# Two gated attention and expert layers on one core: the first layer taken batch by batch, with the rows for the experts scattered in four groups

## The chip, the cores and the metric

The kernel runs on one core of a Trainium2 chip, as one program. The metric is the device time of one execution in microseconds (us), the median of several. All times in this document are microseconds unless another unit stands beside them. Engines: PE (TensorE, matrix multiplies and transposes), DVE (VectorE), ACT (ScalarE), POOL (GpSimd, which here also issues the indirect DMAs), SP (which issues the plain DMAs).

## The reference, cut to what matters

`x` is 4 batches of 256 tokens with 256 features, `ctx` the same tokens with 64 features. Four steps each add a gated term to `x`; `ln` is a layernorm without weights.

```
sim  = (ctx Wq0)(ctx Wk0)^T scaled; keep the 76 largest of each row     # per batch 256 x 256
A    = sigmoid(sim) * kept;  A = (A + A^T) / 2
x   += tanh(g_xattn[0]) * ((1 - gamma) * ln(x) + gamma * A)             # layer 0, attention
y    = for each token t, expert e = t mod 4 (64 tokens of a batch each):
       (silu(ln(x) Wg_e) * (ln(x) Wu_e)) Wd_e                           # 256 -> 256 -> 256
x   += tanh(g_ffn[0]) * y                                               # layer 0, FFN
s    = (ctx Wq1 + bq)(ctx Wk1 + bk)^T / 8 * ln(x); masks; softmax
x   += tanh(g_xattn[1]) * softmax(s)                                    # layer 1, attention
p    = softmax(ln(x) router), 8 best of 64 experts for each token
x   += tanh(g_ffn[1]) * sum over the 8 of weight * expert(ln(x))        # 256 -> 96 -> 256
```

## The kernel before, in words

Everything is float32. A tile is 128 tokens; a batch is two tiles, the whole input eight. Each engine runs its own program in the order in which it is written, and waits on semaphores for the others.

**Up to the first layer.** PE transposes `ctx`, projects it and makes `sim` for all batches. DVE's `keep_top(b)` finds the 76th largest of each row by ten rounds of `max` (8 values, L991) and `match_replace` (L995), two tiles at a time, and masks `adj` (L1000). `mix_adjacencies(b)` (L1016, L1020) adds the transposed `adj` and the input, `statistics(n, b)` (L966 to L972) makes mean and variance. POOL's `inverse_deviation(n, b)` (L439, L441) turns a variance into 1/sqrt and a shift; ACT's `normalise` (L827) applies them; PE's `transpose_normed` (L583) transposes the result, and ACT's `evacuate_xnt` copies it to `xn_t`.

**FFN of layer 0.** It is done in two halves of two batches. `q` counts half and expert, 0 to 7, each with `TE` = 128 tokens of one expert: `expert_gate_up0(q)` (L604) fills a PSUM bank with gate and another with up, ACT makes `silu0` (L847) and copies `up0` (L849), POOL multiplies them into `h0_t` (L449, `up_times_silu`), `expert_down0(q)` (L593) multiplies by the down weights, ACT copies to `y0_t` (L839), PE transposes it back (`transpose_y0`, L615) and DVE's `add_layer0` adds it.

**Layer 1 up to the experts.** DVE's `masked_scores`, ACT's `exp_scores` (L855), DVE's `add_softmax` and `statistics(3, b)`, POOL's deviation, ACT's normalise into `x_rows`, PE's transposes and `router_logits` (L626), ACT's copy, DVE's `choose_experts` (L1066 to L1072), PE's `rank_rows` (L672, L673: how many earlier tokens chose the same expert) and DVE's `place_rows` (L1080 to L1092), which writes for each token and pick the row in DRAM where its features go (`place_at`).

**Scatter.** POOL then sends the rows: 64 indirect DMAs (L478, `place_rows` in POOL's program), each 128 rows of 320 floats to `expert_rows`, 16 for each batch. They wait for `place_ready` of the batch, for `x_rows_ready`, and for `rows_cleared`: SP's one DMA that fills the first 192 rows of each expert with an empty row (L349). SP loads the expert rows (`load_rows`, L361) only when all 64 have landed (`placed`).

**Experts.** 63 times PE transposes the rows of an expert (L704), multiplies by gate and up (L715) and by down (L724), with DVE and ACT between; POOL scatters the results to `token_picks` (L499). At the end PE sums each token's eight picks (L770) and DVE adds them (L1241). SP loads the experts' weights (L355, L356) eight ahead, the first of them after the last scores, since the weights share a buffer with the projections. Ahead of the experts DVE also counts, lists the experts with over 192 tokens (L1157 to L1186), makes the router weights and picks them (L1113).

**Order.** The eight PSUM banks are taken in turn. `fills` lists every use; `begin(i)` makes PE wait until use `i - 8` was emptied, and `filled(i)` makes a reader wait for `bank_filled`, which counts uses in that order. So the order of all work is written out by hand in five places: the list of fills and the four engines' programs. In the order before, DVE takes `keep_top(1)`, batches 0 and 1 mixed, `keep_top(2)`, 2 mixed, `keep_top(3)`, 3 mixed, then layer 0 and the scores of batches 0 and 1, their experts and places, and last the same for 2 and 3. POOL takes all eight products and most deviations ahead of the first scatter:

```python
            place_rows(0, 0, 2)
            inverse_deviation(2, 2)
            place_rows(0, 2, 4)
            inverse_deviation(2, 3)
            place_rows(0, 4, 10)
            inverse_deviation(3, 2)
            place_rows(0, 10, 13)
            inverse_deviation(3, 3)
            place_rows(0, 13, PICKS)
            for b in range(1, B):
                place_rows(b, 0, PICKS)
```

Of the kernel before, what the change touches and what calls it, by code (L numbers as in the profile page):

```python
# [14 lines left out]
P = 128  # L15
# [19 lines left out]
def gated_layers_kernel(nc, x, ctx_in, mask_ss, mask_bs, g_xattn, g_ffn, wq0, wk0, gamma_raw, gate_up, down,  # L35
# [12 lines left out]
    TE = HALF // NE0  # L48
# [17 lines left out]
    with ExitStack() as stack:  # L66
# [118 lines left out]
        evac = {who: sem(who + "_evac") for who in ("act", "dve")}  # L185
# [35 lines left out]
        F_CTX, F_PROJ, F_SIM, F_SCORE = {}, {}, {}, {}  # L221
        F_CTX[0] = add_fill("ctx", "act")
# [9 lines left out]
        for b in range(B):  # L232
            F_SCORE[b] = add_fill("score", "act")


        F_ADJT, F_XNT, F_YT, F_XNT2, F_LOGIT = {}, {}, {}, {}, {}
        F_GATE, F_UP, F_DOWN = {}, {}, {}

        def add_gate_up_fills(q):
            F_GATE[q], F_UP[q] = add_fill("gate", "act"), add_fill("up", "act")  # L240

        def add_down_fill(q):
            F_DOWN[q] = add_fill("down", "act")

        for fill, name, who in ((F_ADJT, "adjt", "dve"), (F_XNT, "xnt", "act")):
            for b in (0, 1):
                fill[b] = add_fill(name, who)
        for q in range(NE0):
            if q == NE0 - 1:
                F_ADJT[2] = add_fill("adjt", "dve")  # L250
            add_gate_up_fills(q)
            if q:
                add_down_fill(q - 1)
        add_down_fill(NE0 - 1)
        F_XNT[2] = add_fill("xnt", "act")
        F_ADJT[3] = add_fill("adjt", "dve")
        F_YT[0], F_YT[1] = add_fill("yt", "dve"), add_fill("yt", "dve")
        F_XNT[3] = add_fill("xnt", "act")
        add_gate_up_fills(NE0)
        for q in range(NE0 + 1, 2 * NE0 - 1):  # L260
            add_gate_up_fills(q)
            add_down_fill(q - 1)
        F_XNT2[0], F_XNT2[1] = add_fill("xnt2", "act"), add_fill("xnt2", "act")
        add_gate_up_fills(2 * NE0 - 1)
        F_LOGIT[0], F_LOGIT[1] = add_fill("logit", "act"), add_fill("logit", "act")
        add_down_fill(2 * NE0 - 2)
        add_down_fill(2 * NE0 - 1)
        F_RANK = {}
        F_RANK[0], F_RANK[1] = add_fill("rank", "dve"), add_fill("rank", "dve")
        F_YT[2], F_YT[3] = add_fill("yt", "dve"), add_fill("yt", "dve")  # L270
        F_XNT2[2], F_LOGIT[2] = add_fill("xnt2", "act"), add_fill("logit", "act")
        F_XNT2[3] = add_fill("xnt2", "act")
        F_RANK[2] = add_fill("rank", "dve")
        F_LOGIT[3] = add_fill("logit", "act")
        F_RANK[3] = add_fill("rank", "dve")
# [13 lines left out]
        LAYERNORMS = ((0, None), (1, 0), (1, 1), (1, 2), (1, 3), (2, 0), (2, 1), (3, 0), (3, 1), (2, 2), (2, 3), (3, 2), (3, 3))  # L289
# [11 lines left out]
        def xn_t_view(k, b, permuted):  # L301

            if permuted:
                return xn_t[:, k].rearrange("p (f e b g) -> p f e b g", f=2, e=NE0, b=B // 2)[:, b // 2, :, b % 2, :]
            return xn_t[:, k, b * S:(b + 1) * S]
# [99 lines left out]
        def _(pool):  # L405
# [37 lines left out]
            def up_times_silu(half, experts):  # L443
                for e in experts:
                    q = half * NE0 + e
                    emptied(pool, F_UP[q])
                    if q >= 2:
                        pool.wait_ge(bank_filled, F_DOWN[q - 2] + 1)
                    pool.tensor_tensor(h0_t[:, q % 2].rearrange("p i t -> p (i t)"), silu0[:, q % 2], up0[:, q % 2],  # L449
                                       ALU.mult).then_inc(h0_ready, 1)  # L450
# [7 lines left out]
            inverse_deviation(1, 0)  # L458
            inverse_deviation(1, 1)
            up_times_silu(0, range(NE0))  # L460
            for n, b in ((1, 2), (1, 3), (2, 0), (2, 1)):
                inverse_deviation(n, b)
            up_times_silu(1, (0,))
            inverse_deviation(3, 0)
            up_times_silu(1, (1,))
            inverse_deviation(3, 1)
            up_times_silu(1, (2, 3))
# [14 lines left out]
            place_rows(0, 0, 2)  # L482
            inverse_deviation(2, 2)
            place_rows(0, 2, 4)
            inverse_deviation(2, 3)
            place_rows(0, 4, 10)
            inverse_deviation(3, 2)
            place_rows(0, 10, 13)
            inverse_deviation(3, 3)
            place_rows(0, 13, PICKS)  # L490
            for b in range(1, B):
                place_rows(b, 0, PICKS)
# [21 lines left out]
        def _(pe):  # L514
# [49 lines left out]
            for b in range(B):  # L564
                query_times_key(1, F_SCORE, b)

# [20 lines left out]
            def expert_down0(q):  # L587
                i = F_DOWN[q]
                begin(i)
                pe.wait_ge(h0_ready, q + 1)  # L590
                for hc in range(KC):
                    for ic in range(IC):
                        last = pe.matmul(bank(i)[:, hc * TE:(hc + 1) * TE], down_w[:, q % NE0, ic, hc * P:(hc + 1) * P],  # L593
                                         h0_t[:, q % 2, ic, :], start=ic == 0, stop=ic == IC - 1)
                last.then_inc(bank_filled, 1)

            def expert_gate_up0(q):
                half, e = q // NE0, q % NE0
                for part, fill in enumerate((F_GATE[q], F_UP[q])):
                    begin(fill)  # L600
                    for ic in range(IC):
                        for k in range(KC):
                            c = part * I0 + ic * P
                            last = pe.matmul(bank(fill)[:, ic * TE:(ic + 1) * TE], gu_w[:, e, k, c:c + P],  # L604
                                             xn_t[:, k, half * HALF + e * TE:half * HALF + (e + 1) * TE], start=k == 0, stop=k == KC - 1)
                    last.then_inc(bank_filled, 1)

            def transpose_y0(b):
                emptied(pe, F_DOWN[b // 2 * NE0 + NE0 - 1])
# [20 lines left out]
            transpose_adj(0)  # L630
            transpose_adj(1)
            transpose_normed(F_XNT, xn, xn_ready, 0)
            transpose_normed(F_XNT, xn, xn_ready, 1)
            pe.wait_ge(ld["gu"], 16 * NE0)
            pe.wait_ge(ld["down"], 16 * NE0)
            emptied(pe, F_XNT[1])
            for q in range(NE0):
                if q == NE0 - 1:
                    transpose_adj(2)
                expert_gate_up0(q)  # L640
                if q:
                    expert_down0(q - 1)
            expert_down0(NE0 - 1)
            transpose_normed(F_XNT, xn, xn_ready, 2)
            transpose_adj(3)
            transpose_y0(0)
            transpose_y0(1)
# [3 lines left out]
            for q in range(NE0 + 1, 2 * NE0 - 1):  # L651
                expert_gate_up0(q)
                expert_down0(q - 1)
# [623 lines left out]
```

## Time and profile before

| what | value |
|---|---|
| median of three runs | 417.0 (415.72 to 417.07) |
| the profiled execution, its own time | 417.87 |
| its span, first to last instruction | 416.1 |
| mean granted clock of PE | 0.844 of full speed |
| PE, DVE, ACT, POOL busy | 275.1, 210.7, 118.0, 214.0 |

The span has three stages: the two layers up to the places, with the row scatters at their end, to 203.4; the experts from 206.5 to 365.6; the sum of the picks from 383.0 on. Averages of busy time mix these, so the stages must be read one by one. In the timeline a line merges alike instructions that follow each other; the brackets at its end give the idle time before it and what ended it.

### The profile page before, as it was taken

Reading aid. Unit: us, or ns where it says so; the run is one execution under the profiler, and the core shown is the slowest. Engines: PE = TensorE matmul, PEld = TensorE weight load, DVE = VectorE, ACT = ScalarE, POOL = GpSimd, SP = SyncE. Lnnn points to the kernel's source line nnn. Section 1 sums busy time; section 2 is a strip of 40 time slices with the busy share of each in tenths; the row PEclk is TensorE's granted clock in tenths of the full one; section 3 lists DMA queues with packets and bytes.
Section 4 is the critical chain, followed back from the end, with each engine's and each line's share of the span. In section 5 each row is a group of like instructions: output and inputs, shape, how many; then the busy total and the mean of one; then the engine's idle time right before and its main releaser. Section 6 shows DMA issues by size and latency. Waiting matters only on the chain.

```text
span 416.1 us, 5526 instructions
## 1 busy us (share of the span) xinstructions
PE 275.1 (66%) x1546; PEld 230.9 (55%) x1546; DVE 210.7 (51%) x921; ACT 118.0 (28%) x265; POOL 214.0 (51%) x256
## 2 busy tenths in 40 slices
PE   5898177137801610000199999999999999951997
PEld 1335067037800500000189999889999889931886
DVE  0799999989386679000033433343433343340352
ACT  2264353316634500000023333333333333320000
POOL 2622112013267777777327777777777777771000
PEclk9999999557975555555589999999999999995899
DMA  4899995360013333333498888888888887226891
GB/s 132 312 352 306 318 310 192 91 190 2 1 63 113 126 126 127 126 127 138 148 243 267 273 270 277 271 264 274 261 273 269 269 270 229 74 73 234 325 305 64
DMA packets 47374, 84.12 MB, mean 202 GB/s; under 512 B 10453, under 2 KB 28249, under 8 KB 46320
## 3 DMA queue, kind: packets, MB, share of 16 engines
q1 hardware_dynamic: 38128, 64.87, 49.9%
q0 software_dynamic: 9216, 18.90, 13.0%
q8 instruction: 13, 0.21, 0.2%
q14 instruction: 17, 0.14, 0.1%
HBM read 48.07 MB, written 39.85 MB: 211 GB/s over the span
## 4 chain that ended last, share of the span: by engine, by line
PE 52%; DVE 18%; POOL 16%; issue 7%; DMA 4%; ACT 2%; SPq 1%; POOLq 1%; ACTq 0%
PE psum L715 20%; POOL expert_rows L478 14%; PE psum L724 13%; PE psum L770 7%; PE psum L704 5%; DVE work L995 5%; DVE top L991 5%; DVE stats L966 2%; PE psum L536 2%; PE psum L530 2%; DMA sim<-token_picks 1%; POOL token_picks L499 1%; PE psum L604 1%; DVE adj L1000 1%; DMA gu_w<-expert_rows 1%
## 5 line engine op out<-in xcount | busy, mean ns | idle before, releaser
L499 POOL DMA_INDIRECT token_picks<-down_w,target x126 | 117.3, 931 | 54.9 <-issue 41.1
L715 PE MATMUL psum<-gu_w,wgu 128*96 128x192 f32 x504 | 93.7, 329 | 0.0
L715 PEld LDWEIGHTS psum<-gu_w,wgu 128*96 128x96 f32 x504 | 78.0, 165 | 0.6 <-DVE gu_w L1203 0.2
L478 POOL DMA_INDIRECT expert_rows<-x_rows,place_at x64 | 62.4, 975 | 23.8 <-issue 23.8
L724 PE MATMUL psum<-proj_t,gu_w 96*96 96x256 f32 x252 | 64.8, 379 | 0.0
L927 ACT ACTIVATE gu_w<-psum 96x192 f32<-96x192 f32 x63 | 20.6, 326 | 130.0 <-PE psum L715 130.0
L1208 DVE TENSOR_TENSOR gu_w<-gu_w,psum 96x192 f32<-96x192 f32 x63 | 22.1, 350 | 67.1 <-ACT gu_w L927 67.1
L704 PE MATMUL psum<-ident,gu_w 96*128 96x96 f32 x108 | 14.1, 256 | 53.1 <-DMA gu_w<-expert_rows 53.1
L933 ACT COPY down_w<-psum 96x512 f32<-96x512 f32 x63 | 36.6, 581 | 33.9 <-PE psum L724 33.9
L724 PEld LDWEIGHTS psum<-proj_t,gu_w 96*96 96x96 f32 x252 | 41.1, 163 | 7.1 <-DVE gu_w L1208 0.4
L704 PEld LDWEIGHTS psum<-ident,gu_w 96*128 96x128 f32 x108 | 12.5, 148 | 57.6 <-DMA gu_w<-expert_rows 54.4
L1203 DVE COPY gu_w<-psum 128x384 f32<-128x384 f32 x63 | 34.4, 547 | 0.0
L439 POOL TENSOR_TENSOR rstd<-var_eps,minus_half 128x2 f32<-128x2 f32 (+1 forms) x13 | 10.4, 797 | 46.6 <-DVE var_eps L972 46.5
L1202 DVE COPY target<-gu_w 96x2 uint32<-96x2 uint32 x27 | 4.5, 165 | 52.6 <-PE psum L704 52.6
L991 DVE MAX8 top<-work 128x8 f32<-128x256 f32 x72 | 26.8, 413 | 0.0
L995 DVE MATCH_REPLACE8 work<-top,work 128x256 f32<-128x256 f32 x64 | 25.7, 409 | 0.0
L604 PE MATMUL psum<-xn_t,gu_w 128*128 128x128 f32 x128 | 19.0, 316 | 1.7 <-ACT xn_t L832 1.7
L604 PEld LDWEIGHTS psum<-xn_t,gu_w 128*128 128x128 f32 x128 | 18.4, 231 | 2.4 <-issue 1.3
L449 POOL TENSOR_TENSOR h_t<-silu,up 128x256 f32<-128x256 f32 x8 | 6.1, 762 | 23.9 <-ACT up L849 23.6
L770 PE MATMUL psum<-sim,xn_t 128*128 128x256 f32 x32 | 9.9, 480 | 11.0 <-DMA sim<-token_picks 11.0
L1241 DVE TENSOR_TENSOR xs<-psum,scores 128x256 f32<-128x256 f32 x8 | 3.4, 424 | 27.3 <-PE psum L770 27.3
L583 PE MATMUL psum<-ident,x_rows 128*128 128x128 f32 x16 | 3.4, 351 | 20.8 <-ACT x_rows L827 19.8
(177 smaller groups left out, 397.1 us busy)
## 6 DMA issues: line engine op xcount, KB each, us to landing
expert_rows<-empty_rows SPq DMA_DIRECT2D x1, 15360.0 KB, 69.3
wgu<-in_L_ffn_w_gate_up SPq DMA_DIRECT2D x65, 192.0 KB, 2.9
gu_w<-expert_rows SPq DMA_DIRECT2D x28, 240.0 KB, 4.2
proj_t<-in_L_ffn_w_down SPq DMA_DIRECT2D x65, 96.0 KB, 4.0
sim<-expert_rows SPq DMA_DIRECT2D x18, 240.0 KB, 4.3
work<-expert_rows SPq DMA_DIRECT2D x18, 240.0 KB, 4.2
gu_w<-in_L_ffn_gate_up_proj SPq DMA_DIRECT2D x4, 512.0 KB, 8.2
sim<-token_picks SPq DMA_DIRECT2D x2, 1024.0 KB, 4.9
```

Of the source, the lines that this page charges most:

```text
L478: pool.indirect_dma_start(rows_dram, bass.IndirectOffsetOnAxis(ap=place_at[:, t, k:k + 1], axis=0), x_rows[:, t, :], None).then_inc(placed ...
L499: pool.indirect_dma_start(picks_dram, bass.IndirectOffsetOnAxis(ap=target[0:SLOTS, e % T_RING, i:i + 1], axis=0), y_slots[0:SLOTS, n, i, : ...
L604: last = pe.matmul(bank(fill)[:, ic * TE:(ic + 1) * TE], gu_w[:, e, k, c:c + P], xn_t[:, k, half * HALF + e * TE:half * HALF + (e + 1) * T ...
L704: last = pe.transpose(psum[:, e % 2, k * CAP + i * SLOTS:k * CAP + (i + 1) * SLOTS], x_slots[n][0:SLOTS, i, k * P:(k + 1) * P], ident[0:SL ...
L715: last = pe.matmul(psum[0:I1, 2 + e % 2, part * CAP:(part + 1) * CAP], wgu[:, n, k, part * I1:(part + 1) * I1], x_slots_t[:, e % 2, k, :], ...
L724: last = pe.matmul(psum[0:SLOTS, 4 + e % 2, i * D:(i + 1) * D], h1_t[:, e % 2, i * SLOTS:(i + 1) * SLOTS], wd[:, n, :], start=True, stop=True)
L770: last = pe.matmul(psum[:, t, 0:D], diag[:, t % 2, k, :], picks[t % K_RING][:, k * D:(k + 1) * D], start=k == 0, stop=k == TOP_K_EXPERTS - 1)
L933: act.copy(y_slots[0:SLOTS, n].rearrange("p i d -> p (i d)"), psum[0:SLOTS, 4 + e % 2, 0:SUBS * D]).then_inc(y_ready, 1)
L991: dve.max(top8[:, t, r], (work if r else sim)[:, t]).then_inc(top8_ready, 1)
L995: dve.match_replace(work[:, t], top8[:, t, r], (work if r else sim)[:, t], REMOVED).then_inc(rest_ready, 1)
L1203: dve.tensor_copy(x_slots_t[:, e % 2].rearrange("p k n -> p (k n)"), psum[:, e % 2, 0:KC * CAP]).then_inc(xt_copied, 1)
L1208: dve.tensor_tensor(h1_t[:, e % 2], silu1[:, e % 2], psum[0:I1, 2 + e % 2, CAP:2 * CAP], ALU.mult).then_inc(h_ready, 1)
```

## The change

The first layer and what follows it is taken batch by batch. `TE` becomes 64: a product, a gate and up and a down are those of one expert in one batch, so there are 16 of each, and gate and up share one PSUM bank, as the four downs of a batch do. `keep_top` of later batches is cut into rounds and spread between the work of earlier batches. The scores of layer 1 are made later, and each kind of bank has an evacuation semaphore of its own. POOL scatters the rows of batch 0 when they are placed, then those of batch 1, 2 and 3, and does deviations and half of the products between them. The product of silu and up stays on POOL throughout. The parts of the diff that set the order:

```diff
-    TE = HALF // NE0
+    TE = S // NE0
...
+        add_fills(("adjt", 0), ("score", 0), ("score", 1), ("xnt", 0), ("score", 2),
+                  ("gu", 0), ("gu", 1), ("gu", 2), ("adjt", 1), ("gu", 3), ("down", 0),
+                  ("score", 3), ("yt", 0), ("xnt", 1),
+                  ("gu", 4), ("gu", 5), ("gu", 6), ("gu", 7), ("down", 1),
+                  ("xnt2", 0), ("logit", 0), ("yt", 1), ("adjt", 2), ("rank", 0), ("xnt", 2),
+                  ("gu", 8), ("gu", 9), ("gu", 10), ("gu", 11), ("down", 2),
+                  ("xnt2", 1), ("logit", 1), ("yt", 2), ("rank", 1), ("adjt", 3), ("xnt", 3),
+                  ("gu", 12), ("gu", 13), ("xnt2", 2), ("gu", 14), ("logit", 2), ("gu", 15), ("rank", 2), ("down", 3),
+                  ("yt", 3), ("xnt2", 3), ("logit", 3), ("rank", 3))
...
+            def up_times_silu(*which):
+                for q in which:
+                    emptied(pool, F_GU[q])
+                    need(pool, down_step, q - 1)
                     pool.tensor_tensor(h0_t[:, q % 2].rearrange("p i t -> p (i t)"), silu0[:, q % 2], up0[:, q % 2],
                                        ALU.mult).then_inc(h0_ready, 1)
...
             inverse_deviation(1, 0)
+            up_times_silu(0, 1, 2, 3)
             inverse_deviation(1, 1)
+            inverse_deviation(2, 0)
+            up_times_silu(4, 5, 6, 7)
             inverse_deviation(3, 0)
+            inverse_deviation(1, 2)
...
             place_rows(0, 0, 2)
+            inverse_deviation(2, 1)
+            place_rows(0, 2, 9)
+            inverse_deviation(3, 1)
+            up_times_silu(8)
+            place_rows(0, 9, 10)
+            up_times_silu(9)
+            place_rows(0, 10, 12)
+            up_times_silu(10)
+            place_rows(0, 12, 14)
+            up_times_silu(11)
+            place_rows(0, 14, PICKS)
+            place_rows(1, 0, 3)
+            inverse_deviation(1, 3)
+            place_rows(1, 3, 5)
             inverse_deviation(2, 2)
+            place_rows(1, 5, 10)
+            inverse_deviation(3, 2)
+            place_rows(1, 10, 11)
+            up_times_silu(12)
+            place_rows(1, 11, 12)
+            up_times_silu(13)
+            place_rows(1, 12, 14)
+            up_times_silu(14)
+            place_rows(1, 14, PICKS)
+            up_times_silu(15)
+            place_rows(2, 0, 3)
             inverse_deviation(2, 3)
+            place_rows(2, 3, 9)
             inverse_deviation(3, 3)
+            place_rows(2, 9, PICKS)
+            place_rows(3, 0, PICKS)
```

PE takes its work in the order of the fills, with `expert_down0` between: `expert_gate_up0(8)`, `(9)`, `expert_down0(8)`, `expert_gate_up0(10)`, `expert_down0(9)`, `expert_gate_up0(11)`, `expert_down0(10)`, `expert_down0(11)`, and the like for the other batches. DVE's new order, and ACT's from batch 0's products on:

```diff
+            keep_top(1, 0, 2)
+            mix_adjacencies(0)
+            statistics(1, 0)
+            keep_top(1, 2, ROUNDS)
+            keep_top(2, 0, 1)
+            mix_adjacencies(1)
+            statistics(1, 1)
+            keep_top(2, 1, 4)
+            add_layer0(0)
+            statistics(2, 0)
+            keep_top(2, 4, 5)
+            masked_scores(0)
+            keep_top(2, 5, 7)
+            softmax_and_statistics(0)
+            keep_top(2, 7, ROUNDS)
+            choose_experts(0)
             mix_adjacencies(2)
             statistics(1, 2)
+            place_rows(0)
+            add_layer0(1)
+            statistics(2, 1)
+            keep_top(3, 0, 1)
+            masked_scores(1)
+            keep_top(3, 1, 2)
+            softmax_and_statistics(1)
+            keep_top(3, 2, 3)
+            keep_top(3, 3, 4)
+            keep_top(3, 4, 6)
+            choose_experts(1)
+            keep_top(3, 6, 7)
+            place_rows(1)
+            keep_top(3, 7, ROUNDS)
+            add_layer0(2)
             mix_adjacencies(3)
             statistics(1, 3)
+            statistics(2, 2)
             masked_scores(2)
+            softmax_and_statistics(2)
+            router_weights(0)
+            router_weights(1)
+            choose_experts(2)
+            place_rows(2)
+            add_layer0(3)
+            statistics(2, 3)
             masked_scores(3)
+            softmax_and_statistics(3)
             choose_experts(3)
             place_rows(3)
...
+            silu_and_up0(0, 1, 2, 3)
+            normalise(1, 1)
+            evacuate_down(0)
+            copy_scaled(scores, F_SCORE, 3, SCORE_SCALE)
+            evacuate_xnt(F_XNT, True, 1)
+            silu_and_up0(4, 5)
             act.preload_act_table(ACT.Exp)
             exp_scores(0)
+            act.preload_act_table(ACT.Silu)
+            silu_and_up0(6, 7)
+            scale_x(2)
+            evacuate_down(1)
+            normalise(3, 0)
+            evacuate_xnt(F_XNT2, False, 0)
+            copy_logits(0)
+            scale_x(3)
+            normalise(1, 2)
+            evacuate_xnt(F_XNT, True, 2)
+            silu_and_up0(8, 9)
+            act.preload_act_table(ACT.Exp)
             exp_scores(1)
             act.preload_act_table(ACT.Silu)
+            silu_and_up0(10, 11)
             normalise(3, 1)
+            evacuate_down(2)
             evacuate_xnt(F_XNT2, False, 1)
             copy_logits(1)
+            normalise(1, 3)
...
```

## Rows read from the trace of the kernel before

**Rows 1.** The chain that ended last: start, length, what

```profile
188.24 0.96 POOL expert_rows L478
...
200.86 2.47 DMA expert_rows<-x_rows,place_at
```

**Rows 2.** Timeline of POOL: start, length, engine, line, tiles, idle before

```profile
110.19 0.73 POOL L449 TENSOR_TENSOR h_t<-silu,up 128x256 f32<-128x256 f32 x1 [3.54 <-ACT up L849]
116.09 1.23 POOL L478 DMA_INDIRECT expert_rows<-x_rows,place_at  x1 [5.18 <-issue]
...
120.33 1.04 POOL L478 DMA_INDIRECT expert_rows<-x_rows,place_at  x1 [0.16 <-issue]
...
123.91 1.04 POOL L478 DMA_INDIRECT expert_rows<-x_rows,place_at  x1 [0.16 <-issue]
```

**Rows 3.** DMA issues: size of one, us from issue to landing

```profile
expert_rows<-empty_rows SPq DMA_DIRECT2D x1, 15360.0 KB, 69.3
```

**Rows 4.** Timeline of SP's queue

```profile
16.19 0.61 SPq L349 DMA_DIRECT2D expert_rows<-empty_rows  x1
40.49 35.63 SPq L355 DMA_DIRECT2D wgu<-in_L_ffn_w_gate_up  x1
```

**Rows 5.** Timeline of DVE: the first instruction of each step named, and the last pick

```profile
32.81 0.75 DVE L991 MAX8 top<-sim 128x8 f32<-128x256 f32 x2
...
47.35 0.68 DVE L1016 TENSOR_TENSOR adj<-adj,psum 128x512 f32<-128x512 f32 x1
...
52.80 0.74 DVE L991 MAX8 top<-sim 128x8 f32<-128x256 f32 x2
...
89.82 0.74 DVE L1025 SCALAR_TENSOR_TENSOR xs<-psum,tg,xs 128x512 f32<-128x512 f32 x1
...
93.82 0.88 DVE L1034 SCALAR_TENSOR_TENSOR work<-xs,mv,scores 128x256 f32<-128x256 f32 x2
...
97.55 0.16 DVE L1047 TENSOR_SCALAR live<-row_max 128x2 f32<-128x2 f32 x1
...
100.92 0.17 DVE L1047 TENSOR_SCALAR live<-row_max 128x2 f32<-128x2 f32 x1
...
110.87 0.36 DVE L1066 MAX8 l_top<-logits 128x8 f32<-128x64 f32 x2 [6.27 <-ACT logits L860]
...
113.10 0.47 DVE L1080 TENSOR_TENSOR_SCAN order<-chosen,zeros 128x64 f32<-128x64 bf16 x2
...
115.05 0.47 DVE L1080 TENSOR_TENSOR_SCAN order<-chosen,zeros 128x64 f32<-128x64 bf16 x2
...
146.98 0.30 DVE L1157 COPY counts<-psum 128x64 f32<-128x64 f32 x1
...
166.53 0.21 DVE L1113 SCALAR_TENSOR_TENSOR xn<-order,rw 128x64 f32<-128x64 f32 x1
```

**Rows 6.** Timeline of PE: gate and up, router, down; and router later

```profile
107.75 1.95 PE L604 MATMUL psum<-xn_t,gu_w 128*128 128x128 f32 x16
109.53 1.90 PE L626 MATMUL psum<-router,xn_t 128*128 128x64 f32 x16
111.27 2.00 PE L593 MATMUL psum<-h_t,down_w 128*128 128x128 f32 x16
...
140.38 1.95 PE L626 MATMUL psum<-router,xn_t 128*128 128x64 f32 x8
```

**Rows 7.** Timeline of ACT: batch 3 normalised for the router

```profile
137.20 1.09 ACT L827 ACTIVATE x_rows<-xs,shift,rstd 128x256 f32<-128x256 f32 x2 [0.96 <-POOL shift L441]
```

**Rows 8.** Windows: busy PE, PEld, DVE, ACT, POOL, PE clock, DMA share, GB/s

```profile
41.00:73.00 32.00, 16.72 (x112) 15.12 (x112) 30.69 (x115) 13.40 (x32) 5.96 (x10) 1.00 0.84 272
119.00:134.00 15.00, 0.33 (x2) 0.35 (x3) 11.85 (x53) 5.24 (x14) 11.92 (x16) 0.50 0.27 99
145.00:165.00 20.00, 2.13 (x12) 0.86 (x9) 16.97 (x157) 1.12 (x1) 15.43 (x16) 0.50 0.36 132
175.00:195.00 20.00, 0.00 (x0) 0.00 (x0) 0.00 (x0) 0.00 (x0) 15.12 (x17) 0.50 0.35 127
```

More of the change, by code:

```diff
@@ L248, in gated_layers_kernel @@
[L248 to L262, printed above, removed]
@@ L871, in finish_x3 @@
                     act.activation(x3[:, t], xs[:, t], ACT.Identity, bias=dead_nan[:, t:t + 1]).then_inc(x3_ready, 1)
-            for b in (0, 1):
-                normalise(1, b)
-            for b in (0, 1):
-                evacuate_xnt(F_XNT, True, b)
-            for q in range(NE0):
-                silu_and_up0(q)
-                if q:
-                    evacuate_down(q - 1)
-            evacuate_down(NE0 - 1)
+            sigmoids(0)
+            act.wait_ge(ld["bias"], 32)
+            for w in (2, 3):
+                for half in range(2):
+                    copy_projection(w, half)
@@ new lines, in _ @@
+            sigmoids(1)
+            scale_x(0)
+            copy_scaled(scores, F_SCORE, 0, SCORE_SCALE)
+            copy_scaled(scores, F_SCORE, 1, SCORE_SCALE)
+            normalise(1, 0)
+            evacuate_xnt(F_XNT, True, 0)
+            sigmoids(2)
+            sigmoids(3)
+            act.preload_act_table(ACT.Silu)
+            copy_scaled(scores, F_SCORE, 2, SCORE_SCALE)
+            scale_x(1)
+            silu_and_up0(0, 1, 2, 3)
+            normalise(1, 1)
+            evacuate_down(0)
@@ L980, in _, with keep_top @@
                               ALU.mult).then_inc(evac["dve"], 1)
-            def keep_top(b):
+            def keep_top(b, first, end):
                 emptied(dve, F_SIM[b])
                 tiles = range(b * HB, (b + 1) * HB)
-                for r in range(ROUNDS):
+                for r in range(first, end):
                     for t in tiles:
@@ L1115, in pick_weights, with softmax_and_statistics @@
                 link(last)
[L1117 to L1121 removed]
+            def softmax_and_statistics(b):
+                add_softmax(b)
+                statistics(3, b)
+            keep_top(1, 0, 2)
[5 more added lines that the diff above has]
+            statistics(1, 1)
@@ L1125, in _ @@
+            keep_top(3, 1, 2)
[8 more added lines that the diff above has]
+            add_layer0(2)
             mix_adjacencies(3)
             statistics(1, 3)
-            for b in (0, 1):
-                add_layer0(b)
-                statistics(2, b)
-            dve.wait_ge(pen_ready, NT)
@@ L1131, in _ @@
-            emptied(dve, F_SCORE[B - 1])
-            masked_scores(0)
-            masked_scores(1)
-            for b in (0, 1):
-                add_softmax(b)
-                statistics(3, b)
-            choose_experts(0)
-            choose_experts(1)
-            place_rows(0)
-            place_rows(1)
-            for b in (2, 3):
-                add_layer0(b)
-                statistics(2, b)
-            masked_scores(2)
-            masked_scores(3)
-            for b in (2, 3):
-                add_softmax(b)
-                statistics(3, b)
```

288 lines of the change are left out of this document (131 added, 157 removed).

## The prediction

> **What bounds the kernel now.** I read the chain that ended last first, then each engine's timeline along it. The chain runs through POOL's indirect DMAs without a break: the last of the 64 row scatters starts at 200.86, its rows land 2.47 later, and eleven starts, 188.24 to 200.86, are 1.262 apart [rows 1]. POOL's timeline shows the first at 116.09 [rows 2]. No expert can run before the last has landed, so in this stage POOL sets the time, and what follows 200.86 is the same in both kernels. The DVE timeline shows what gates the first scatter: `choose_experts(0)` at 110.87 sat idle 6.27 for logits, and its batch could not come earlier because all four `keep_top` and two batches of everything else are queued ahead [rows 5]. DVE has done its last `pick_weights` at 166.7 and then waits for POOL.
>
> So I work out one number: the start of the last scatter. It moves the end one for one.
>
> **When the first scatter can start.** DVE leaves the common part at 32.81. Differences of starts give each function: `keep_top` 14.54 (ten rounds, 1.45 each), mix and statistics 2.73, `add_layer0` and statistics 2.00, masked scores 1.87, softmax and statistics 3.37, `choose_experts` 1.12, `place_rows` 1.95 [rows 5]. Ahead of `place_rows(0)`'s end the new order has two `keep_top`, three mixes, and one of each other: 29.1+8.2+2.0+1.9+3.4+1.1+2.0 = 47.6, so 80.4; I add 1.3 for adjacency transposes and logits that DVE will meet late: 81.7. PE does not hold it: DVE has batch 0's first statistics at 32.8+2.9+2.7 = 38.4, POOL, ACT and PE need 4 for deviation, normalise, transposes and copy, so PE's first gate and up starts near 44, and its twice as long FFNs have DVE's `keep_top(1)` and `keep_top(2)` as cover.
> POOL, however, also waits for `rows_cleared`: the 15.36 MB clear is issued at 16.19 [rows 4] and lands 69.3 later [rows 3], at 85.5. This wait was free before and is now the gate. The first scatter began 1.04 after `place_rows(0)` had ended (116.09 against 115.05) [rows 2, 5]; I take 1.0 for each first scatter behind a wait (bound 0.3: 1.262 less the 0.96 that a scatter lasts [rows 1]). First scatter: 86.5, some 29.6 earlier.
>
> **POOL's own work from there.** 63 steps of 1.262 are 79.5. Seven `inverse_deviation` lie between (four before): from 120.33 to 123.91 are two scatters and one pair, so a pair adds 1.06 [rows 2], 7.4 in all. Eight of the sixteen products lie between too. The 128x256 product takes 0.73 [rows 2], the new one is 128x128; between 0 and 0.73 I take 0.45, 3.6 (bounds 0 and 5.8). Sum: 86.5+79.5+7.4+3.6 = 177.0 if POOL never waits.
>
> **Where POOL will wait.** The products and deviations of later batches stand in POOL's queue between the scatters of batches 0 and 1. PE, ACT and DVE wait for those, and then POOL for them: the transposes and logits of batch 1 stand in PE's queue behind the whole FFN of batch 2 (products 8 to 11), ACT's normalise of them behind silu 11; ranks and logits of batch 2 stand among the FFN of batch 3 (12 to 15).
> Width first. An FFN product works on 64 tokens, not 128, and there are 16. The 128x64 router matmuls take 111.27-109.53 = 1.74 for 16, the 128x128 gate and up matmuls ahead 1.78 for 16 [rows 6]: with 128 weight columns half the width costs the same. PE thus does twice the FFN time: 1.75 for a gate and up, 0.9 for a down, at the high clock; 8 router matmuls at the low clock take 1.95 [rows 6], so twice that there. PE held 2.4 GHz through 41 to 73 at half its time busy, and showed 1.2 GHz after it had stopped, 119 to 134 [rows 8]. From PE's end to a finished product are 110.92-109.6 = 1.3 [rows 2, 6].
> - *Ahead of batch 1's rows.* POOL reaches product 8 after nine scatters and two pairs: 86.5+11.4+2.1 = 100.0. Batch 2's first statistics end at 79.7 (ahead of `place_rows(0)`), its transposes by 83, gate and up 8 and 9 by 87.5; then PE is idle, so it starts at 1.2 GHz: down 8 and gate and up 10 end at 105.1, product 10 is ready at 105.7 where POOL came at 104.5: wait 1.2. Product 11 at 109.2, down 11 at 110.2, then transposes, copy, logits, copy 2.8: `choose_experts(1)` at 113.0 (DVE idle since 102), one round, `place_rows(1)` ends 117.5. POOL is through batch 0 at 112.0 and resumes at 118.5: wait 6.5.
> - *Ahead of batch 3's first deviation.* POOL takes three scatters (to 122.0) and then wants `inverse_deviation(1,3)`: DVE has 4.5 of `keep_top(3)`, 0.8, PE's low-clock transposes, mix and statistics, to 125.9: wait 4.0.
> - *Ahead of batch 2's rows.* Thirteen scatters, three pairs and four products take POOL to 147.4. Meanwhile down 12, transposes, gate and up 14, down 13, logits, gate and up 15, down 14 and ranks follow product 12 (139.5) in PE: ranks at 148.1, `place_rows(2)` at 149.2, first scatter 150.2: wait 2.8.
> - *Ahead of batch 3's rows.* Sixteen scatters and two pairs: 172.5. The rows of batch 3 follow `inverse_deviation(3,3)` (163.4): before, ACT's normalise at 137.20 to `place_rows(3)`'s end at 146.98 was 9.8 [rows 5, 7], of it 1.0 `router_weights`: 172.2, start 173.2: wait 0.7.
> Together 15.2. Last scatter at 192.2, 8.7 earlier than 200.86.
>
> **What is hidden.** The tail that DVE does after `place_rows(3)` was 146.98 to 166.7, 19.8 [rows 5]; now it ends near 192, and the expert rows can reach PE no sooner than 192.2+2.5+3.1 = 197.8, so 5.8 are left. If the last batch's placing came over 5.8 late without POOL, DVE would be the bound. Four ACT table loads more lie in ACT's slack: ahead of exponentials they run while DVE does a round or more of `keep_top`, ahead of silu 10 while PE waits for product 8 (cover gone, each would add its length once). SP's weight loads now wait for the last scores (near 58); before, SP's first of them hung 35.6 from 40.49, until 76 [rows 4], behind the clear, so the later wait costs nothing. The extra wait of PE for its own down matmul is 0.1 or 0.2 four times, and nothing is gained or lost in the expert loop.
>
> The profiled execution took 417.87, the median is 417.0. 417.87-8.7 = 409.2, less 0.9: **408.3**.
>
> **Port rule.** Scatters beside a busy DVE (145 to 165, DVE 16.97) and beside an idle one (175 to 195) fill POOL alike, 15.43 and 15.12 [rows 8]; at most 0.3 in 16, so I add nothing. The new kernel puts `keep_top` beside scatters, of which no row tells; were each of about 30 scatters held by one `max` of 0.37 (0.75 for two [rows 5]), 11 would be added, part of it inside the waits.
> The Trainium skill, SBUF — State Buffer, "SBUF: two separate sides", says that VectorE in a two-port mode locks GpSimd out of writing descriptors. By that rule the overlap would cost; by the rows it does not.
>
> **The rivals.**
> - *Half width is half the time.* Against: the equal 1.74 and 1.78. For: the router's weights were another tile. Gate and up 0.9 and down 0.45 would remove the 1.2, some 3.5 of the chain to batch 1's rows and the 2.8 ahead of batch 2's: 7.5, time 400.8. The Trainium skill, TensorE: Matmul & The Clock Gate, "Back-to-back issue gap", has the isolated gap grow with the width, and says that a stream with weight loads is paced by both; the first formula gives this rival, the rows go with the second.
> - *POOL hardly waits* (shorter latencies, scatters resuming after 0.3): 177.0 is the floor, 23.9 earlier, 393.
> - *PE stays at 1.2 GHz whenever it is fed through POOL.* Place: product 8 to `choose_experts(1)` and product 12 to `place_rows(2)`. For: PE is busy in bursts with gaps of a scatter or two, as it was before it fell. Against: half busy was enough at 41 to 73. Price: the 8 of PE work between product 8 and logits 1 doubles, less 2 already counted, 6; the 8.3 from down 12 to ranks doubles: 14.3. That eats the 8.7: **slower**, 422.6. It decides once the waits exceed 15.2+8.7 = 23.9.
> - *Partly that*: one of the two bursts low, 6 to 8 lost: 414 to 416, hardly a gain.
>
> **How the numbers follow.** A measurement here can tell 0.3% (1.25) from no change. Forecast's branch, 403 to 413: 0.55. Half width or few waits, 392 to 403: 0.20. The partial case, 413 to 418.3: 0.13, of it 0.06 within 0.3% and 0.07 faster. Low clock, above: 0.12. Faster 0.82, same 0.06, slower 0.12. The range leaves out the deepest part of the second and the last: 399 to 417.5.
>
> **What the changed profile would show.** First scatter of batch 0 at 86.5, held by the clear and not by `place_at`; eight products of about 0.45 among the scatters; 16 gate and up groups of 1.75; POOL idle of about 6.5, 4 and 3 ahead of batch 1's first scatter, `inverse_deviation(1,3)` and batch 2's first scatter; the last scatter at 192, first expert transposes at 198. Wrong if DVE and PE deliver batches 1 and 2 more than a few microseconds later or earlier than worked out, or if the clear lands at another time: the end follows that one for one.

## The result, and the profile after

| | median | lowest to highest | runs |
|---|---|---|---|
| before | 416.72 | 415.72 to 417.07 | 4 |
| after | 442.41 | 441.31 to 446.19 | 4 |

The ratio is 1.0637, with a 95% interval from 1.0568 to 1.0706: the change makes the kernel 6% slower, where 2% faster was forecast. The profiled execution took 441.57, its span is 439.8 (416.1 before).

The timeline of POOL in the kernel after, where the first scatter of each batch, the last one, and the waits stand:

```profile
101.50 0.78 POOL L414 TENSOR_TENSOR rstd<-var_eps,minus_half 128x2 f32<-128x2 f32 x1 [12.12 <-DVE var_eps L1004]
...
104.32 1.24 POOL L448 DMA_INDIRECT expert_rows<-x_rows,place_at  x1 [1.75 <-issue]
...
144.36 0.96 POOL L448 DMA_INDIRECT expert_rows<-x_rows,place_at  x1 [9.78 <-issue]
...
152.30 0.72 POOL L414 TENSOR_TENSOR rstd<-var_eps,minus_half 128x2 f32<-128x2 f32 x1 [4.44 <-DVE var_eps L1004]
...
179.54 0.45 POOL L422 TENSOR_TENSOR h_t<-silu,up 128x128 f32<-128x128 f32 x1 [3.95 <-ACT up L860]
183.31 1.01 POOL L448 DMA_INDIRECT expert_rows<-x_rows,place_at  x1 [3.31 <-issue]
...
206.99 0.96 POOL L448 DMA_INDIRECT expert_rows<-x_rows,place_at  x1 [0.93 <-issue]
...
226.25 0.96 POOL L448 DMA_INDIRECT expert_rows<-x_rows,place_at  x1 [0.30 <-issue]
```

The last scatter starts at 226.25, 25.4 later than before and 34.1 later than the 192.2 of the forecast. The lateness is there from the first scatter on (17.8 behind the forecast's 86.5) and grows in each batch that has an FFN ahead of it. What follows the last scatter takes nearly the same in both kernels: 439.8 - 226.25 = 213.6 against 416.1 - 200.86 = 215.2. In the timeline of DVE after, whose steps the forecast added up for batch 0, DVE sits idle for logits ahead of `choose_experts` of batches 0, 1 and 2:

```profile
97.20 0.35 DVE L1101 MAX8 l_top<-logits 128x8 f32<-128x64 f32 x2 [9.32 <-ACT logits L871]
...
138.99 0.35 DVE L1101 MAX8 l_top<-logits 128x8 f32<-128x64 f32 x2 [14.20 <-ACT logits L871]
...
175.91 0.35 DVE L1101 MAX8 l_top<-logits 128x8 f32<-128x64 f32 x2 [10.58 <-ACT logits L871]
```

The logits come from PE behind the FFN. The timeline of PE after, for batch 0 and then around batch 2's FFN and batch 1's logits (L598 is gate and up, L584 down, L620 the router; a float32 matmul stands in the trace as two records, so x16 is one gate and up, of eight matmuls, and x8 one down; "matmul" with a count or a pace means such a record from here on):

```profile
43.81 7.09 PE L598 MATMUL psum<-xn_t,gu_w 128*128 128x64 f32 x32
50.69 1.91 PE L584 MATMUL psum<-h_t,down_w 128*128 128x64 f32 x8
52.40 3.62 PE L598 MATMUL psum<-xn_t,gu_w 128*128 128x64 f32 x16
...
97.51 1.06 PE L561 MATMUL psum<-ident,adj 128*128 128x128 f32 x4
...
105.66 7.09 PE L598 MATMUL psum<-xn_t,gu_w 128*128 128x64 f32 x32 [0.73 <-ACT xn_t L845]
120.67 1.94 PE L584 MATMUL psum<-h_t,down_w 128*128 128x64 f32 x8 [7.93 <-POOL h_t L422]
122.41 3.62 PE L598 MATMUL psum<-xn_t,gu_w 128*128 128x64 f32 x16
...
136.69 1.97 PE L620 MATMUL psum<-router,xn_t 128*128 128x64 f32 x8 [0.74 <-ACT xn_t L845]
```

A gate and up takes 3.41 from its start to that of the down behind it (52.40 to 55.81), not 1.75; a down takes 1.71 (50.69 to 52.40), not 0.9. A matmul takes 3.41 / 16 = 0.213. This is the pace that the 8 router matmuls had in the kernel before at a granted clock of 0.50 (1.95, [rows 6]); here the same 8 take 1.97. So PE runs at the lower of its two levels, 1.2 GHz. It does so from its first FFN matmul, and four 128x128 transposes at 97.51 still take 1.06.

The granted clock recorded for the same stretches says otherwise. Windows of the kernel after (busy PE, PEld, DVE, ACT, POOL, then clock, DMA share, GB/s):

```profile
43.00:66.00 23.00, 22.85 (x104) 21.95 (x103) 15.49 (x60) 6.87 (x18) 2.67 (x6) 1.00 0.92 305
```

PE is busy 22.85 of 23.00 and the record says full speed, but only 104 matmuls pass. The mean over the span is 0.988, against 0.844 before: read by the record, the slower kernel had the better clock. The chain of work that ended last gives the time on it by line: L598 11.0% and L584 6.3% of 439.8 are 76. The Trainium skill warns of exactly this record (TensorE: Matmul & The Clock Gate, "Seeing it yourself": clock events in a trace have been seen to be unreliable on this chip). The trace agrees: 1.00 beside 0.213 per matmul.

### The profile page after: what moved, and what is told of

It is laid out like the page before. It is cut to its first block, busy times and chain, and to the rows that moved or that the text cites. A ratio compares the mean times of both kernels' runs of the same rounds, so it can differ in the third digit from the quotient of the medians.

```text
span 439.8 us, 5963 instructions
## 1 busy us (share of the span) xinstructions
PE 336.0 (76%) x1738; PEld 290.2 (66%) x1738; DVE 212.0 (48%) x921; ACT 124.3 (28%) x277; POOL 213.5 (49%) x264
## 4 chain that ended last, share of the span: by engine, by line
PE 68%; DVE 10%; POOL 10%; issue 5%; DMA 3%; ACT 3%; SPq 1%; POOLq 0%; PEldq 0%; DVEq 0%; ACTq 0%
PE psum L733 19%; PE psum L742 12%; PE psum L598 11%; POOL expert_rows L448 7%; PE psum L788 7%; PE psum L584 6%; PE psum L722 5%; DVE work L1026 2%; DVE top L1022 2%; PE psum L571 2%; POOL rstd L414 2%; DVE stats L998 1%; PE psum L527 1%; PE psum L620 1%; DMA sim<-token_picks 1%
## 5 line engine op out<-in xcount | busy, mean ns | idle before, releaser
L490 POOL DMA_INDIRECT token_picks<-down_w,target x126 | 115.5, 917 | 55.4 <-issue 41.0
L598 PE MATMUL psum<-xn_t,gu_w 128*128 128x64 f32 x256 | 57.1, 421 | 2.2 <-ACT xn_t L845 2.2
L598 PEld LDWEIGHTS psum<-xn_t,gu_w 128*128 128x128 f32 x256 | 55.9, 332 | 4.1 <-ACT xn_t L845 3.4
L584 PE MATMUL psum<-h_t,down_w 128*128 128x64 f32 x128 | 30.1, 422 | 10.5 <-POOL h_t L422 10.5
L584 PEld LDWEIGHTS psum<-h_t,down_w 128*128 128x128 f32 x128 | 28.8, 332 | 10.8 <-issue 10.8
L422 POOL TENSOR_TENSOR h_t<-silu,up 128x128 f32<-128x128 f32 x16 | 7.3, 456 | 47.3 <-ACT up L860 47.2
L1101 DVE MAX8 l_top<-logits 128x8 f32<-128x64 f32 x8 | 1.4, 218 | 41.8 <-ACT logits L871 41.8
L859 ACT ACTIVATE silu<-psum 128x128 f32<-128x128 f32 x16 | 4.4, 278 | 53.5 <-PE psum L598 53.5
```

What stands on the lines that cost most here:

```text
L490: pool.indirect_dma_start(picks_dram, bass.IndirectOffsetOnAxis(ap=target[0:SLOTS, e % T_RING, i:i + 1], axis=0), y_slots[0:SLOTS, n, i, : ...
L584: last = pe.matmul(bank(i)[:, c:c + TE], down_w[:, e, ic, hc * P:(hc + 1) * P], h0_t[:, q % 2, ic, :], start=ic == 0, stop=ic == IC - 1)
L598: last = pe.matmul(bank(F_GU[q])[:, at:at + TE], gu_w[:, e, k, c:c + P], xn_t[:, k, b * S + e * TE:b * S + (e + 1) * TE], start=k == 0, st ...
```

## The experiments

All are ratios to the kernel before, timed on the same chip. "Wide" below means that each FFN matmul is fed its 64 columns twice, so 128 pass through and the second half is overwritten or not read; the number of instructions stays the same. (In the downs this is done wherever the doubled output still fits its bank.)

**Is it the width? (e1_wide, e2_before_narrow)**

```diff
-    last = pe.matmul(bank(F_GU[q])[:, at:at + TE], gu_w[:, e, k, c:c + P],
-                     xn_t[:, k, b * S + e * TE:b * S + (e + 1) * TE], ...)
+    last = pe.matmul(bank(F_GU[q])[:, at:at + 2 * TE], gu_w[:, e, k, c:c + P],
+                     twice(xn_t[:, k, b * S + e * TE:b * S + (e + 1) * TE]), ...)
```

> The changed kernel, with each FFN matmul of layer 0 fed its 64 columns twice (128 moving columns, the second copy written to PSUM where it is overwritten or not read): same instructions, same waits, same results. Theory A (the 64-column stream leaves PE at 1.2 GHz, and that is the whole loss): gate and up of 16 falls from 3.41 to about 1.8, down from 1.7 to 0.9, the row scatters begin near 86.5 (the clear) in place of 104.3, and the time is 404 to 414. Theory B (the pace of 213 ns is that of loading 128 weight columns, whatever streams): nothing changes, 442. Theory C (queueing behind POOL is most of the loss, PE's pace a lesser part): gate and up gets faster, but the time stays above 425.

Measured: 411.79, ratio 0.9878 (0.9841 to 0.9914). Work was added to PE and the time fell by 30.6. The timeline of PE in e1_wide:

```profile
43.71 5.38 PE L602 MATMUL psum<-xn_t,gu_w 128*128 128x128 f32 x32
48.93 1.06 PE L588 MATMUL psum<-h_t,down_w 128*128 128x128 f32 x8
49.83 1.95 PE L602 MATMUL psum<-xn_t,gu_w 128*128 128x128 f32 x16
```

The pace changes within the first 32 matmuls (5.38 lies between the 7.09 of the narrow ones and twice 1.8), and from there a gate and up is 1.8. POOL's timeline in e1_wide follows the forecast wait by wait (the forecast had 1.2 ahead of product 10, then 6.5, 4.0 and 2.8):

```profile
85.89 1.23 POOL L448 DMA_INDIRECT expert_rows<-x_rows,place_at  x1 [1.76 <-issue]
...
106.38 0.45 POOL L422 TENSOR_TENSOR h_t<-silu,up 128x128 f32<-128x128 f32 x1 [1.37 <-ACT up L864]
...
119.45 0.95 POOL L448 DMA_INDIRECT expert_rows<-x_rows,place_at  x1 [7.26 <-issue]
127.37 0.72 POOL L414 TENSOR_TENSOR rstd<-var_eps,minus_half 128x2 f32<-128x2 f32 x1 [4.45 <-DVE var_eps L1008]
...
152.92 1.01 POOL L448 DMA_INDIRECT expert_rows<-x_rows,place_at  x1 [2.23 <-issue]
```

The reverse edit takes the kernel before and feeds only the first 64 of each 128 tokens to its FFN matmuls; the other half of layer 0's FFN is left out (`y0_t` holds zeros there, from one more POOL instruction at the start, and ACT's copies into it are half as wide).

```diff
-    last = pe.matmul(bank(fill)[:, ic * TE:(ic + 1) * TE], ..., xn_t[:, k, at0:at0 + TE], ...)
+    last = pe.matmul(bank(fill)[:, ic * TE:ic * TE + TE // 2], ..., xn_t[:, k, at0:at0 + TE // 2], ...)
```

> The kernel before, with its FFN of layer 0 done for only the first 64 of each 128 tokens (64 moving columns, the same number of matmuls; the other tokens get no FFN term in layer 0). Half the columns, same instructions. Theory A: PE never leaves 1.2 GHz before the scatters, each gate and up of 16 takes 3.4 in place of 1.8, the second half's FFN (94 to 113 before) takes some 15 longer, and the kernel is 3 to 5% slower than before though it does less. Theory B (width costs nothing, clock as before): same time, 416 to 418, gate and up 1.8. Theory that half width is half the time: gate and up 0.9, 3 to 8 us faster.

Measured: 427.66, ratio 1.0245 (1.0183 to 1.0307), less than the 3 to 5% expected. With half the columns it is 10 slower: the first scatter moves from 116.09 to 127.19, with PE's timeline in e2_before_narrow showing the low pace:

```profile
56.95 7.06 PE L605 MATMUL psum<-xn_t,gu_w 128*128 128x64 f32 x32 [0.93 <-ACT xn_t L833]
...
65.51 3.62 PE L605 MATMUL psum<-xn_t,gu_w 128*128 128x64 f32 x16
```

So the width does it, in the old order as in the new one, and the order itself is not to blame. This run also shows how little the recorded clock says: three executions have a mean of 0.984 and the fourth 0.839, and that one took 426.87 where the profiled one of the three took 427.55.

**Is a narrow matmul slow, or the engine's state? (e5_narrow_filler, e6_first_two_wide)** In e5 the FFN matmuls stay narrow, and one matmul of 512 columns whose result is overwritten goes ahead of each gate and up. In e6 only the gate and up of experts 0 and 1 in each batch are wide.

```diff
                 begin(F_GU[q])
+                pe.matmul(bank(F_GU[q]), ident[:], gu_w[:, e, 0, 0:BANK], start=True, stop=True)   # e5
...
+                twice(rows) if e < 2 else rows                                                    # e6
```

> The changed kernel, its FFN matmuls 64 columns wide as they were, with one 512-column matmul of useless work ahead of each gate and up (16 in all, written where the gate is written next). Theory A (the clock): PE gets to 2.4 GHz in spite of the narrow matmuls; a gate and up of 16 then takes about 1.75 at the unchanged width, and the kernel is faster than the changed one though it does more: 410 to 430. Theory B (narrow matmuls are slow in themselves, 213 ns whatever the clock): gate and up stays 3.4, each filler adds 0.4 to 0.9, 445 to 455.

> The changed kernel with doubled columns for the gate and up of experts 0 and 1 of each batch alone; experts 2 and 3 and all downs stay 64 wide. If the clock, once up, holds under narrow matmuls: all later FFN work of a batch at the fast pace, 410 to 418, as with all doubled. If narrow work lets it fall at once: 425 to 438.

Measured: e5 430.83, ratio 1.0393 (1.0312 to 1.0475); e6 423.07, ratio 1.0174 (1.0113 to 1.0234). PE in e5_narrow_filler, in the course of batch 0:

```profile
50.78 2.81 PE L603 MATMUL psum<-xn_t,gu_w 128*128 128x64 f32 x16
...
54.32 1.08 PE L577 MATMUL psum<-gu_w,ident 128*128 128x512 f32 x2
55.23 1.89 PE L603 MATMUL psum<-xn_t,gu_w 128*128 128x64 f32 x16
```

and in e6_first_two_wide, right behind wide ones and after a stop:

```profile
67.74 1.95 PE L602 MATMUL psum<-xn_t,gu_w 128*128 128x64 f32 x16
...
102.53 1.94 PE L587 MATMUL psum<-h_t,down_w 128*128 128x64 f32 x8 [7.74 <-POOL h_t L422]
104.25 3.62 PE L602 MATMUL psum<-xn_t,gu_w 128*128 128x64 f32 x16
```

The same narrow group takes 1.89 to 1.95 when wide work has brought the engine up, and 3.62 after it stood idle 7.74. So a 64-column matmul is as cheap as a 128-column one at equal level; what narrow work does not do here is bring the level up.

Nor did it hold the level in e6. The last two gate and ups of batch 0 and its downs are narrow there, PE stops at most 0.90 up to batch 1, and batch 1's first stream, which is wide in both runs, takes 5.46 in e6 and 3.84 in e1 (e6_first_two_wide, then e1_wide):

```profile
61.60 5.46 PE L602 MATMUL psum<-xn_t,gu_w 128*128 128x128 f32 x32 [0.73 <-ACT xn_t L849]
```

```profile
60.99 3.84 PE L602 MATMUL psum<-xn_t,gu_w 128*128 128x128 f32 x32 [0.74 <-ACT xn_t L849]
```

Neither version beats the kernel before: e5 pays for each filler, 1.8 at the low level and 0.9 at the high one, and its gate and ups of batches 2 and 3 are in part slow again (3.51 at 152.34); e6 is low from batch 1's first stream, and again when POOL makes PE stop in the later batches. The times fall outside what was expected for them: e5 lies 0.8 above its 410 to 430, e6 between its two cases.

**What POOL's queue adds (e3_dve_products, e4_wide_dve).** The products of batches 2 and 3 move to DVE, in e3 with the change's narrow matmuls and in e4 with wide ones.

```diff
+            products(8, 9)          # DVE, behind keep_top(3, 1, 2)
+            products(10)            # behind (3, 2, 3)
+            products(11)            # behind (3, 3, 4)
+            products(12, 13, 14)    # ahead of choose_experts(2)
+            products(15)            # behind it
```

> The changed kernel with the products 8 to 15 on DVE instead of in POOL's queue between the scatters. Theory A (PE's pace is the loss): PE waits for a product behind POOL only twice, 10.5 in all, so 5 to 12 us faster, 430 to 437, not near 417. Theory C (queueing behind POOL): 20 or more faster, below 422.

> The two edits together: doubled columns and products 8 to 15 on DVE. Theory A: PE fast, and no product behind a scatter; the waits that the prediction put ahead of batch 1's and 2's rows (6.5 and 2.8) shrink, 398 to 408, a few us below the doubled columns alone. If DVE's own queue takes POOL's place as what holds the products, no better than the doubled columns alone.

Measured: e3 433.2, ratio 1.0382 (1.032 to 1.0443); e4 406.22, ratio 0.9725 (0.9664 to 0.9786). Taking the product off POOL is worth 9.2 at the low level and 5.6 at the high one. The width costs 30.6 (the change against e1), so the product's place is not the main cause.

**A version that beats both (e7_early_top).** In e4 POOL still waited 4.44 for `inverse_deviation(1, 3)`, behind `keep_top(3)`. e7 is e4 with the last rounds of `keep_top(3)` ahead of `choose_experts(1)`, where DVE sat idle, and product 11 one round later. Against the kernel after:

```diff
-            keep_top(3, 4, 6)
-            choose_experts(1)
-            keep_top(3, 6, 7)
-            place_rows(1)
-            keep_top(3, 7, ROUNDS)
+            keep_top(3, 4, 5)
+            products(11)
+            keep_top(3, 5, ROUNDS)
+            choose_experts(1)
+            place_rows(1)
```

> Doubled columns and DVE products as before, and the last rounds of keep_top(3) ahead of choose_experts(1), in the time in which DVE waits for its logits. The wait of POOL ahead of batch 3's first deviation (4.4 in the run before) should shrink to about 1, its FFN and batch 2's rows come 3 to 4 earlier: 401 to 404, against 406. If it only moves: batch 1's rows come 1 to 2 later and nothing is won.

Measured: 402.77, ratio 0.9678 (0.9648 to 0.9709), the fastest of all. In its POOL timeline the wait for that deviation is gone, and the first scatter is at last held by the clear (issued at 16.1, landing 68.2 later at 84.3):

```profile
84.58 1.23 POOL L450 DMA_INDIRECT expert_rows<-x_rows,place_at  x1 [2.47 <-DMA expert_rows<-empty_rows]
...
113.67 0.95 POOL L450 DMA_INDIRECT expert_rows<-x_rows,place_at  x1 [6.16 <-issue]
```

**Keeping PE up through its stops (e8_warm, e10_warm_mended, e9_end_filler, e12_end_filler_again, e11_early_top_again).** All are e7 with useless 512-column matmuls on PE: e8 5 ahead of the transposes of batches 2 and of 3, 24 ahead of batch 3's last ones and 36 ahead of the experts; e10 has 5, 5, 14 and 18 there; e9 and e12 only the last 18. e11 is e7 once more, beside e12.

```diff
+            filler(psum[:, 6, :], 36, down_w[:, 0].rearrange("p i d -> p (i d)"))   # e8; 18 in the others
```

> The same, and useless 512-column matmuls in PE's long waits (5 each ahead of the transposes of batches 2 and 3, 24 ahead of the router transposes of batch 3, 36 ahead of the expert loop), so that PE is at 2.4 GHz when the work comes. Theory A: gate and up 8 and 12 and the first expert at the fast pace, 2 to 3 from the expert loop's start and 2 to 5 from the chain of batches 2 and 3: 395 to 400. If the fillers last too long they delay what follows, and it is slower than without.

> Doubled columns, products 8 to 15 on DVE and early keep_top as in the version before, and 18 useless 512-column matmuls (of 0.92 each) at the end of PE's wait for the expert rows, to end some 3 before they come. Theory A: the first expert is transposed and multiplied at 2.4 GHz, 1.5 to 2.5 faster: 398 to 401 against 402.8. If they outlast the wait, slower by what they are over; if PE has fallen back in the gap, the same time.

> The same, and fillers in the earlier waits too, cut to end within them (5 ahead of the transposes of batches 2 and 3, 14 ahead of the router transposes of batch 3). Theory A: another 1 to 3 from the chains of batches 2 and 3: 396 to 400. If POOL's own work is the floor by now, no better than the fillers at the end alone.

> The kernel of the run with early keep_top again, to stand on one chip beside the one with fillers at the end: the last two runs were on a chip where the kernel before took 476.7, and can't be compared with 402.8. Ratio to before 0.965 to 0.970 as it was, if this chip is like the first.

> With the 18 fillers ahead of the expert loop. Theory A: 1.5 to 2.5 us faster than the run beside it. If PE falls back in the gap after the fillers, or they gain nothing: the same within 1.

| | time | ratio (95%) | before there |
|---|---|---|---|
| e8 | 418.17 | 1.004 (1.002 to 1.0059) | 416.72 |
| e9 | 458.15 | 0.9589 (0.9528 to 0.9649) | 476.73 |
| e10 | 463.6 | 0.9694 (0.9644 to 0.9745) | 476.73 |
| e11 | 458.19 | 0.9599 (0.9551 to 0.9646) | 478.13 |
| e12 | 458.85 | 0.959 (0.9534 to 0.9646) | 478.13 |

e8 was mis-sized. The 36 matmuls of 512 columns (x72) take 33.19, 0.92 each, and PE's timeline has them in front of rows that were due near 194 (the last scatter starts at 188.62, and in e7 the rows reach PE 5.5 after that start):

```profile
175.95 33.19 PE L582 MATMUL psum<-down_w,ident 128*128 128x512 f32 x72 [1.08 <-DVE over_void L1263]
208.98 0.83 PE L739 MATMUL psum<-ident,gu_w 96*128 96x96 f32 x8
```

With 18 the filler ends before the rows come (e12's first transposes stand at 194.19, 0.48 behind it), and e12 against e11 is 0.959 against 0.9599: nothing that can be measured. The PE timelines of both (e11, then e12, whose profiled execution took 462.18 against a median of 458.85) suggest why. The first expert's gate and up waits for DVE in each and runs at the low pace, in e12 although the transposes ahead of that wait were fast (0.55 for x4; in e11 1.71 for x8):

```profile
200.83 2.87 PE L739 MATMUL psum<-gu_w,wgu 128*96 128x192 f32 x8 [4.00 <-DVE gu_w L1269]
```

```profile
201.28 2.87 PE L741 MATMUL psum<-gu_w,wgu 128*96 128x192 f32 x8 [5.70 <-DVE gu_w L1271]
```

e10 against e9 is slower by 5.5, so the fillers between batches cost more than they give; 1.9 of it are there at the last scatter (190.47 against 188.58), and where the rest arises was not followed up. The gains that were expected of fillers, 3 to 8 for e8 and 1 to 3 each for the others, are seen in none of the comparisons on one chip, and e11's ratio lies a little below the 0.965 to 0.970 expected. On a chip where the kernel before takes 417 the last 18 were not tried.

## Why the prediction was wrong

The starts that the prediction worked out, beside those of four kernels:

| scatter start | forecast | after | e1 | e4 | e7 |
|---|---|---|---|---|---|
| batch 0 | 86.5 | 104.32 | 85.89 | 86.89 | 84.58 |
| batch 1 | 118.5 | 144.36 | 119.45 | 115.44 | 113.67 |
| batch 2 | 150.2 | 183.31 | 152.92 | 148.59 | 142.42 |
| batch 3 | 173.2 | 206.99 | 175.88 | 171.52 | 165.35 |
| last | 192.2 | 226.25 | 195.22 | 190.87 | 184.68 |

**The step that failed** is "PE thus does twice the FFN time: 1.75 for a gate and up, 0.9 for a down, at the high clock", and with it "PE does not hold it" for batch 0. Measured are 3.41 and 1.71. Over 16 of each that is 16 x 1.66 + 16 x 0.81 = 39.5 more of PE than at the high level throughout; the forecast had put only a down and a gate and up of batch 2 at the low one. With the level put back in e1 the last scatter starts at 195.22: 31.0 of the 34.1 are the level, and the other 3.0 are in e1 too. The step rested on "PE held 2.4 GHz through 41 to 73 at half its time busy" [rows 8]. That sentence fails twice. The new kernel did better than half busy, 22.85 of 23.00, and stays low all the same. And the record did not show the level. Three rows of PE's timeline and one window of the kernel before, which could have been read beforehand:

```profile
52.86 1.09 PE L583 MATMUL psum<-ident,xn 128*128 128x128 f32 x4 [4.19 <-ACT xn L827]
57.23 5.44 PE L604 MATMUL psum<-xn_t,gu_w 128*128 128x128 f32 x32 [0.93 <-ACT xn_t L832]
...
67.56 0.63 PE L573 MATMUL psum<-ident,adj 128*128 128x128 f32 x4 [1.32 <-DVE adj L1000]
```

```profile
46.00:57.20 11.20, 3.26 (x12) 2.15 (x13) 10.88 (x39) 3.56 (x9) 2.16 (x4) 1.00 1.01 334
```

The same four transposes take 1.09 at 52.86 and 0.63 at 67.56, under a recorded 1.00 both times; between them lies a wide stream of 32 that takes 5.44, much of it still at the low level (32 of them take 3.84 in e1 at 60.99). The kernel before entered its FFN low and was brought up in its 128-column stream; with 64 columns in the same place, e2, it was not. In the new order e1 takes 5.38 and the narrow kernel 7.09.

**Right at equal level:** "with 128 weight columns half the width costs the same". e6 has 1.95 for 16 narrow ones, e1 the same for 16 wide ones. But the two rows compared [rows 6] were both taken behind wide work. Width had no price per matmul and a large one in the level that it leaves.

**The rival that came nearest** is "PE stays at 1.2 GHz whenever it is fed through POOL", with a chance of 0.12. Its mechanism was the level, but its cause (stops between products) and its place (from product 8) were too narrow: it priced 14.3 from product 8 on, and the level was low from batch 0, which alone cost 17.8; the 422.6 it gave is still 19.8 short. Stops do count: in e1, all wide, four transposes take 1.08 at 74.62 behind a stop of 2.26, and a down 2.05 at 100.98 behind one of 7.96. But e1 has these stops and gains the 30.6 all the same. "Half width is half the time" is refuted by e6.

**Right, as e1 shows with the level put back:** POOL's own work, the product (0.456 in the mean for 0.45), the 1.262 between scatters also beside `keep_top` (in e7 the scatters from 100.23 to 105.29 start 1.26 or 1.27 apart with rounds of it running throughout), so these instructions of DVE cost the scatters nothing that can be read here; the waits of 7.26, 4.45, 2.23 and 1.37 for 6.5, 4.0, 2.8 and 1.2; the last scatter 3.0 late, the time 411.79 for 408.3. Of the 3.0, 1.6 arise between the first scatters of batches 0 and 1 (33.6 for 32.0), 1.8 between those of batches 1 and 2 (33.5 for 31.7) and 0.3 later; the first scatter gave 0.6 back.

**Right in part by luck:** the first scatter, 85.89 in e1 for 86.5. The forecast had `place_rows(0)` end at 81.7 and the clear land at 85.5 and gate. In e1 the clear landed at 84.3 and `place_rows(0)` ended at 84.94, 3.2 late, and the scatter followed that by 0.95. Two misses offset each other: a DVE path reckoned too short, and a clear that came earlier than reckoned.

**Partly right:** the clear as the gate. It landed at 85.2 in the kernel after, when batch 0's places were still 18 away, and is seen as the gate only in e7. There the scatter began 0.3 after it had landed, not 1.0. The cover of 5.8 for DVE's tail held wherever the kernel before takes 417. In e11 and e12 it was gone: the first expert's gate and up waited for DVE.

## What to carry to other kernels

Halving the moving width of a float32 matmul with 128 weight columns from 128 to 64 saved nothing per matmul here, and it left TensorE at its lower level for a whole stage, however busy it looked; before cutting a batch in two, ask what brought the level up in the old order and whether the new one still does that. Judge the level by the duration of like instructions at several places (four transposes at 1.09 or 0.63), never by the recorded clock alone. If the narrow order is wanted for other reasons, feed the columns twice: that turned 6.4% slower into 1.2% faster, and with half the products on DVE and some rounds of `keep_top` earlier into 3.2% faster.

## What the runs showed of the hardware

- A stream that keeps PE busy 22.85 of 23.00 stayed at the low level when its matmuls were 64 columns wide and rose within its first 32 records when they were 128 wide. The Trainium skill (TensorE: Matmul & The Clock Gate, "What's actually happening") has the level follow how busy PE has been; by the profile's busy time this trace does not bear that out. What the chip counts is not shown by these runs.
- Narrow matmuls right behind wide ones run at the high pace (e6, 67.74). After PE had stood for 7.74 they run at the low one, and there the recorded clock agrees with the pace (0.50 in e6 from 102 to 112), unlike in the kernel after. With narrow groups between, the level had fallen by the next stream though PE stopped no longer than 0.90 (e6, 5.46 at 61.60).
- VectorE's `max` and `match_replace` running beside them leave the starts of GpSimd's indirect DMAs 1.26 or 1.27 apart (e7, 100.23 to 105.29).
- The same kernel takes 417 on some chips and 477 on others. The windows of e11 and then of the kernel after, in the expert stage that both have alike, show where: PE is busy 32.41 of 40.00 at 198 GB/s in e11, and 40.00 at 272 in the kernel after on a chip of the first kind. What makes those chips slower is open.

```profile
260.00:300.00 40.00, 32.41 (x199) 27.64 (x198) 11.69 (x37) 10.94 (x26) 21.62 (x24) 1.00 0.68 198
```

```profile
260.00:300.00 40.00, 40.00 (x258) 36.24 (x257) 15.60 (x50) 14.57 (x33) 29.33 (x33) 1.00 0.89 272
```
